# Layer 1 of a two-layer cross-attention network: probabilities laid out by head, and the prototype bias as a stacked half-precision pair

## The reference

```
x = x + tanh(g_xattn[1]) * attention(layernorm(x), ctx)   # 16 heads of 64, softmax over 77 keys
x = x + tanh(g_ffn[1]) * prototypes(layernorm(x))

def prototypes(x):                       # 32 prototypes, rank 16
    d2 = |x|^2 + |p|^2 - 2 x p^T ;  dists = sqrt(max(d2, 0))
    w = softmax(-dists / t) ;  topw, topi = top_k(w, 2) ;  topw = topw / sum(topw)
    for slot in 0, 1:
        out += topw[slot] * (A[topi[slot]] (B[topi[slot]] x) + bias[topi[slot]])
```

## Time and profile before

| | |
|---|---|
| median of three executions | 3541.69 us |
| the profiled execution | 3538.43 us |
| its span, first to last instruction | 3536.7 us |
| mean granted TensorE clock | 0.972 of full |
| TensorE busy | 3098.9 us, 88% |
| VectorE busy | 2804.7 us, 79% |
| ACT busy | 1992.0 us, 56% |
| GpSimd busy | 1969.2 us, 56% |
| last phase | from about 1819 us to the end |

### The profile page before, as it was taken

The page is one execution under the profiler, slowest core; times in us unless marked ns, Lnnn a source line. Parts: engine busy times, 40 slices in busy tenths (PEclk is TensorE's granted clock), DMA queues, the critical chain, the costliest instruction groups (busy, mean ns, idle before and its releaser), DMA issues. The chain is left out here.

```text
span 3536.7 us, 107677 instructions
## 1 busy us (share of the span) xinstructions
PE 3098.9 (88%) x35590; PEld 2626.6 (74%) x35590; DVE 2804.7 (79%) x6978; ACT 1992.0 (56%) x4103; POOL 1969.2 (56%) x3561
## 2 busy tenths in 40 slices
PE   3999994888888885999958999999999999999997
PEld 2666663666666664999947888888888888888886
DVE  5777774888888886665538898888888888888896
ACT  2666663777777774554525545555455554555553
POOL 0000003666666662000017888888888888888887
PEclk8999996999999997999979999999999999999999
DMA  3665663222232223111022323333233332333331
GB/s 118 274 247 236 248 251 98 77 82 76 75 85 76 75 82 104 36 39 48 3 67 88 99 87 100 89 96 91 88 103 89 99 90 87 103 89 99 89 88 50
DMA packets 352441, 364.00 MB, mean 103 GB/s; under 512 B 109953, under 2 KB 332673, under 8 KB 347137
## 3 DMA queue, kind: packets, MB, share of 16 engines
q1 hardware_dynamic: 338944, 333.23, 29.7%
q10 hardware_dynamic: 12960, 25.23, 1.9%
q0 software_dynamic: 160, 0.52, 0.1%
HBM read 213.11 MB, written 145.78 MB: 101 GB/s over the span
## 5 line engine op out<-in xcount | busy, mean ns | idle before, releaser
L365 POOL TENSOR_TENSOR a_probT_lo<-a_expT,a_probT_hi 128x512 f16<-128x512 f32 (+1 forms) x384 | 372.0, 997 | 244.2 <-ACT a_probT_hi L433 244.2
L933 POOL TENSOR_TENSOR a_pn<-a_prob,a_rsum 128x1232 f32<-128x1232 f32 x128 | 360.0, 2813 | 6.4 <-DVE a_rsum L1273 6.4
L1031 ACT ACTIVATE a_qT_hi<-banks 128x512 f16<-128x512 f32 x256 | 152.8, 597 | 359.0 <-PE banks L140 359.0
L138 PE MATMUL banks<-a_vo,a_probT_hi 128*128 128x256 f16 x1280 | 349.0, 273 | 2.7 <-DVE a_probT_lo L1246 2.6
L140 PE MATMUL banks<-a_vo,a_probT_lo 128*128 128x256 f16 x1280 | 348.9, 273 | 0.0
L139 PE MATMUL banks<-a_vo,a_probT_hi 128*128 128x256 f16 x1280 | 348.9, 273 | 0.0
L424 ACT ACTIVATE a_expT<-banks,a_top,w_score_scale 128x512 f32<-128x512 f32 (+1 forms) x384 | 272.2, 709 | 111.3 <-PE banks L519 111.3
L138 PE MATMUL banks<-a_xnT_hi,w_q_hi 128*128 128x256 f16 x1024 | 282.3, 276 | 4.7 <-DVE a_xnT_lo L1244 4.5
L139 PE MATMUL banks<-a_xnT_lo,w_q_hi 128*128 128x256 f16 x1024 | 282.1, 276 | 0.0
L140 PE MATMUL banks<-a_xnT_hi,w_q_lo 128*128 128x256 f16 x1024 | 282.1, 275 | 0.0
L1967 POOL PARTITION_ALL_REDUCE w_tops<-w_part_tops x1 | 0.4, 367 | 497.6 <-DVE w_part_tops L1994 497.6
(11 more groups left out here) (346 smaller groups left out, 12309.8 us busy)
## 6 DMA issues: line engine op xcount, KB each, us to landing
vo<-kv_vo_out SPq DMA_DIRECT2D x38, 2048.0 KB, 6.5
a_vo<-vo SPq DMA_DIRECT2D x64, 1152.0 KB, 5.8
kt<-kv_k_out ACTq DMA_DIRECT2D x9, 2560.0 KB, 14.6
a_k<-kt SPq DMA_DIRECT2D x64, 308.0 KB, 3.4
a_x<-in_x SPq DMA_DIRECT2D x64, 256.0 KB, 3.0
a_y<-in_x SPq DMA_DIRECT2D x64, 256.0 KB, 2.7
x<-a_y SPq DMA_DIRECT2D x64, 256.0 KB, 2.2
moe_raw<-in_L_ffn_w SPq DMA_DIRECT2D x16, 1024.0 KB, 7.4
```

The source lines that it names most:

```text
L138: nc.tensor.matmul(out, lhs[0], rhs[0], start=start, stop=False)
L365: pool.tensor_tensor(probT[b][1][0:rows, first:end, :], expT[b][0:rows, first:end, :], probT[b][0][0:rows, first:end, :], ALU.subtract).th ...
L933: pool.tensor_tensor(by_key(pn[h]), by_key(prob_of(u, h, 2)), rsum[h][:, :].unsqueeze(1).broadcast_to([P, KEYS, H]), ALU.mult).then_inc(pn ...
L1031: act.activation(out, bank[:, 0:cols].rearrange("p (c s) -> p c s", c=out.shape[1]), ACT.Copy, scale=scale)\
```

## The change

Three things are done.

1. **By head.** `prob` and `pn` hold, head after head, the first 64 keys (`first_keys`), and behind them, head after head, the last 13 (`last_keys`). The shift takes four instructions for two, `normalise` two for one; `softmax_sums` folds 64 keys to 32 and to 16 and adds the last 13, so that `quarter` has 16 x 16 elements for 19 x 16, in runs. The chunks are eight of 128 rows (two heads x 64 keys) and two of 104 rows (eight heads x 13 keys); there are no padding rows and no memsets for them. The values of a batch are loaded in two transfers of 64 partitions and eight of 13.
2. **The bias.** `wsel` is written three times side by side (96 columns), and its transpose `wselT` is in half precision: rows 0 to 63 the high half twice, rows 64 to 95 the low half, by a new subtraction on VectorE between `dots` and `add_residual`. The bias weights are a stack of high, low and high half, also 96 rows. The product is one in half precision. `layer1_weights` prepares the stack and includes the bias in the common scale.
3. **The order.** The transpose of `wsel` stands ahead of the product with the values, on TensorE and in the list of `uses`.

```diff
-            names += of(3, [("out", h)])
             names += of(7, [("wselT", h)])
+            names += of(3, [("out", h)])
...
-    by_key = lambda tile: tile[:, 0:SC].rearrange("p (k h) -> p k h", h=H)
+    first_keys = lambda tile: tile[:, 0:H * FRONT].rearrange("p (h k) -> p h k", h=H)
+    last_keys = lambda tile: tile[:, H * FRONT:SC].rearrange("p (h k) -> p h k", h=H)
...
-            sp.dma_start(vo_sb[p][:, 0:WHOLE, :, :], values(i, 0, WHOLE * P).rearrange("(c p) k d -> p c k d", p=P))\
-                .then_inc(vo_in[p], 16)
-            sp.dma_start(vo_sb[p][0:LEFT, WHOLE, :, :], values(i, WHOLE * P, LEFT)).then_inc(vo_in[p], 16)
+            for a in range(2):
+                sp.dma_start(vo_front[p][a * FRONT:(a + 1) * FRONT, :, :, :], values_front(i, a)).then_inc(vo_in[p], 16)
+            for n in range(MAIN):
+                sp.dma_start(vo_back[p][n * BACK:(n + 1) * BACK, :, :, :], values_back(i, n)).then_inc(vo_in[p], 16)
...
-            pool.tensor_tensor(by_key(pn[h]), by_key(prob_of(u, h, 2)),
-                               rsum[h][:, :].unsqueeze(1).broadcast_to([P, KEYS, H]), ALU.mult).then_inc(pn_ready, 1)
+            for keys_of, n in ((first_keys, FRONT), (last_keys, BACK)):
+                last = pool.tensor_tensor(keys_of(pn[h]), keys_of(prob_of(u, h, 2)),
+                                          rsum[h][:, :].unsqueeze(2).broadcast_to([P, H, n]), ALU.mult)
+            last.then_inc(pn_ready, 1)
...
-                if live(t - 3, NT):
-                    attend(i, t - 3, h, u, j)
                 if live(t - 7, NT):
                     need(pe, wsel_ready, t - 6)
                     bank = bank_for(i, ("wselT", h))
                     filled(nc.tensor.transpose(bank[:, 0:P], wsel[:, :], ident[:, :]), i, ("wselT", h))
+                if live(t - 3, NT):
+                    attend(i, t - 3, h, u, j)
...
-            nc.vector.reduce_sum(rsum[h][:, :], quarter[h][:, :, :].rearrange("p k h -> p h k"), AX.X).then_inc(summed, 1)
+            nc.vector.reduce_sum(rsum[h][:, :], quarter[h][:, :, :], AX.X).then_inc(summed, 1)
...
+                if live(t - 7, NT):
+                    bank, rows = full(i, ("wselT", h)), slice(2 * NPROTO, BIAS_ROWS)
+                    need(dve, wselT_hi, t - 6)
+                    nc.vector.tensor_tensor(wselT[rows, :], bank[rows, 0:P], wselT[rows, :], ALU.subtract)\
+                        .then_inc(wselT_ready, 1)
...
-                    nc.vector.tensor_tensor(wsel[:, 0:NPROTO], pick[:, 0, :], pick[:, 1, :], ALU.add)\
+                    nc.vector.tensor_tensor(wsel[:, 0:BIAS_ROWS].rearrange("p (r n) -> p r n", r=3),
+                                            pick[:, 0, :].unsqueeze(1).broadcast_to([P, 3, NPROTO]),
+                                            pick[:, 1, :].unsqueeze(1).broadcast_to([P, 3, NPROTO]), ALU.add)\
```

More of the change, by code:

```diff
@@ L731, in attention_ffn_phase @@
     rsum = [sb(f"rsum{p}", [P, H]) for p in range(2)]
-    half = sb("half", [P, 2 * QK, H])
-    quarter = [sb(f"quarter{p}", [P, QK, H]) for p in range(2)]
+    half = sb("half", [P, H, FRONT // 2])
+    quarter = [sb(f"quarter{p}", [P, H, FRONT // 4]) for p in range(2)]
     y_sb = [sb(f"y{s}", [P, D]) for s in range(SLOTS)]
@@ L1028, in split_hi @@
         def split_hi(i, use, out, cols, done, scale=1.0):
-            bank = full(i, use)
+            bank = full(i, use)[0:out.shape[0], :]
             act.activation(out, bank[:, 0:cols].rearrange("p (c s) -> p c s", c=out.shape[1]), ACT.Copy, scale=scale)\
@@ L1056, in body @@
                     if live(t - 3, NT):
-                        split_hi(i, ("probT", h, g), probT[0][:, first:end, :], (end - first) * P, probT_hi, PROB_TOP)
+                        split_hi(i, ("probT", h, g), probT[0][0:HEIGHT[g], first:end, :], (end - first) * P, probT_hi,
+                                 PROB_TOP)
                     if g == 0:
@@ L1079, in body @@
                     bank = full(i, ("wselT", h))
-                    act.activation(wselT[:, :], bank[:, 0:P], ACT.Copy).then_inc(wselT_ready, 1)
+                    act.activation(wselT[:, :], bank[0:BIAS_ROWS, 0:P], ACT.Copy).then_inc(wselT_hi, 1)
                 prep(2)
@@ L1149, in turn_probabilities @@
             first, end = GROUPS[g]
-            for c in range(first, end):
-                last = nc.tensor.transpose(bank[:, (c - first) * P:(c - first + 1) * P],
-                                           pn[1 - h][:, c * P:(c + 1) * P], ident[:, :])
+            rows = HEIGHT[g]
+            at = 0 if first < MAIN else MAIN * P
+            for c in range(end - first):
+                place = at + (first % MAIN + c) * rows
+                last = nc.tensor.transpose(bank[0:rows, c * P:(c + 1) * P], pn[1 - h][:, place:place + rows], ident[:, :])
             filled(last, i, ("probT", h, g))
@@ L1158, in attend @@
             need(pe, probT_ready, (t + 1) * PG)
-            need(pe, vo_in[p], (before + 1) * 32)
+            need(pe, vo_in[p], (before + 1) * VALUE_LOADS)
             bank = bank_for(i, ("out", h))
             for c in range(CHUNKS):
-                last = matmul3(nc, bank[:, 0:D], [x[:, c, :] for x in probT], [vo_sb[p][:, c, k, :] for k in range(2)],
+                rows = P if c < MAIN else MAIN * BACK
+                value = vo_front[p][:, c, :, :] if c < MAIN else vo_back[p][:, c - MAIN, :, :]
+                last = matmul3(nc, bank[:, 0:D], [x[0:rows, c, :] for x in probT], [value[:, k, :] for k in range(2)],
                                c == 0, c == CHUNKS - 1)
@@ L1284, in shift_scores @@
             need(dve, pn_ready, t - PROBS + 1)
[L1285 to L1290, removed]
+            tile = prob_of(u, h, 0)
+            for keys_of, first, end in ((first_keys, 0, FRONT), (last_keys, FRONT, KEYS)):
+                out, n = keys_of(tile), end - first
+                nc.vector.tensor_tensor(out[:, 0:2 * held, :].rearrange("p (b h) k -> p b h k", b=2),
+                                        both[:, :, :, first:end],
+                                        both_max.unsqueeze(3).broadcast_to([P, 2, held, n]), ALU.subtract)
+                last = nc.vector.tensor_tensor(out[:, 2 * held:H, :], third[:, :, first:end],
+                                               third_max.unsqueeze(2).broadcast_to([P, BANK_HEADS[2], n]), ALU.subtract)
+            last.then_inc(scores_read, 1)
         def prototype_products(i, t, h):
@@ L1346, in body @@
                     if live(t - 3, NT):
[L1347 to L1348 removed]
+                        split_lo(i, ("probT", h, g), probT[0][0:HEIGHT[g], first:end, :],
+                                 probT[1][0:HEIGHT[g], first:end, :], (end - first) * P, probT_hi, (t - 3) * PG + g + 1, probT_ready, PROB_TOP)
                     if g == 0:
@@ L2426, in flamingo_layers @@
                 ins["L1_ffn_B"], ins["L1_ffn_A"], ins["L1_ffn_bias"], ins["L1_ffn_temp"])
-            attention_ffn_phase(nc, layer, psum, const, batches(x1), tiles(x1), tiles(out), keys(DC, KV_COLS // P), values_out, wq, score_scale,
+            attention_ffn_phase(nc, layer, psum, const, batches(x1), tiles(x1), tiles(out), keys(DC, KV_COLS // P), (out_front, out_back), wq, score_scale,
                                 ffn)
```

88 lines of the change are left out of this document (50 added, 38 removed).

## The result

The changed kernel takes 3560.33 us (median of 3 runs, 3560.3 to 3564.03) against 3541.69: a ratio of 1.0059, 95% interval 1.0036 to 1.0081. It is slower by about 19 us. (In the later runs the kernel before had medians of 3538.6 to 3539.3, against which it would be 21.) The profiled execution took 3560.33 us with a span of 3558.5.

A forecast was written before the change was run, and what follows sets the result against it. Each batch has one stretch limited by VectorE and one by TensorE. Per batch +0.55 - 0.32 = +0.23 us, times 59 = +13.6, on 3538.4 gives 3552; the median shown is 3.3 higher, so about 3555 us, own range 3542 to 3576.

The forecast's parts named there:

- The deciding step: TensorE, h = 0: `out` takes over the bank of `xnT`, so values wait for `xnT_lo`; `yn` 0.55 us later per batch.
- The chain to `xnT_lo`: VectorE's work up to the low half of `xnT`: `rsum` 0.26 shorter, `wsel` 0.07 longer, ending at 2607.47.
- only one of two bias products counts: The bias product of h = 0 saves 0.32 us per batch; that of h = 1 only lengthens TensorE's wait, saving nothing.
- The latency from `xnT_lo` to TensorE: From the end of `xnT_lo` to the first waiting product: 0.06 us taken; 0.15 was seen after `dots`.
- the prediction's sign: In every h = 0 step the first product with the values starts 1.1 to 1.2 us after the last of `low`.
- The ends: Setup before the batches costs +1 us; at the end GpSimd may give back 1.
- GpSimd's part: Sums and `normalise` on GpSimd change by -0.15 to +0.35 us a tile, within its 1.5 us wait per batch; counted as nothing.
- SP's eight issues: Eight more issues for the values at 0.38 us add 3 us to SP's queue; no cost in time.
- That the wait doesn't hold TensorE: Rival: the wait for `xnT` does not hold TensorE; -0.84 us per batch, 3492 us; chance 0.12.
- the 50 computed: The gain if no wait for `xnT` holds TensorE: -0.84 x 59 = -50 us, giving 3492 us.
- That the two cancel: Rival: VectorE's chain is some 0.2 us shorter, so loss and gain cancel; within 7 us of 3542; chance 0.12.
- GpSimd and the values: Two rivals: GpSimd becomes the bound, about 3620 us, chance 0.05; the values come late, 3850 us, chance 0.03.

The follow-up runs named there:

- an earlier `xnT_lo`: The changed kernel, its order kept, with VectorE splitting `xnT` ahead of the maximum of the scores: 3496.83 us, ratio 0.9876.
- the pair of experiments: The changed kernel with three more bias products in each step h = 1: 3562.54 us; then in each step h = 0 instead: 3580.02 us.
- four kernels of four batches: Kernels with four batches written out in layer 1's hardware loop: before 3541.69 us, order alone 3586.50, `xnT_lo` earlier in the kernel before 3538.50, by head alone 3503.87.

## Why the prediction was right

**What held.** The deciding step: with the two uses swapped, the product with the values takes over the bank of `xnT`, once a batch, and costs more than the rest gives. Taking the order back gains 57 us, the order alone costs 47, and an earlier `xnT_lo` gives all of it back. The chain to `xnT_lo` was summed at 7.68 us behind `up` (2607.47 - 2599.79) and measured at 7.67. The parts: shift 0.95 + 0.42 + 0.31 + 0.20 = 1.88 for 1.87, `rsum` 0.41 for 0.41, `wsel` 0.25 for 0.25, the low half of `wselT` (in the prediction that of the bias weights) 0.29 for 0.28, the bias product 0.11 for 0.11. The thirty products with the values and the twelve of `q` took 4.59 for 4.58. That only one of two bias products counts was shown by the pair of experiments.

**Terms that were mis-sized.** The latency from `xnT_lo` to TensorE, taken as 0.06 from the earlier trace rows, was 0.15; the prediction had that value too, behind `dots`, and took the other. So the values start 1.26 us later and not 1.18 (1.25 behind the last product of `low`, where the prediction's sign was 1.1 to 1.2), and a batch costs 0.27 to 0.29 us and not 0.23: over 45 batches +12 us for 10.

**A term left out.** The loop's jumps. The 13 turns were counted like any batch, 13 x 0.23 = 3 us; they went from 28.02 to 28.61, 8 us. The timeline of one ordinary batch can't show it. The ends were set at nothing (+1 - 1) and came to +2. Sum for the profiled execution: 12 + 8 + 2 = 22, against 3560.3 - 3538.4 = 21.9, where 13.6 were forecast. By the medians it is 18.6, since the profiled execution before was 3.3 below its median. So the forecast of 3555 is 5 us off, and like for like it is 8: the mechanism was right and the loss was forecast too small, by terms that all err in the same direction.

**Bounds.** GpSimd's part was to change by -0.15 to +0.35 us a tile; it changed by (2.442 + 2.599) - (2.813 + 2.530) = -0.30, outside on the harmless side, and only its wait grew. `normalise` costs 1902 / 1024 = 1.86 ns an element. The Trainium skill (GPSIMD Engine Reference, section 3.1) gives 4497 / 2048 = 2.20 for a two-input `tensor_tensor` add, held back by a read port that both inputs share. By its shared port an operand that is broadcast would not be cheaper; here it was: a further element cost (1902 - 540) / 816 = 1.67 ns in `normalise`, and (1273 - 732) / 256 = 2.11 in the sums, which read two full operands, in runs too.

SP's eight issues took 8 us of its queue and not 3. They stayed hidden, as the run by head alone shows. The Trainium skill (DMA: Bandwidth & Descriptors, Rules for kernel authors) says that under 64 KB a transfer is mostly overhead; the data queue's share agrees, 33.4% for 29.7% with hardly more bytes, but this share sets nothing here.

**The rivals.** That the wait doesn't hold TensorE was wrong in the changed kernel; its price is what the order put back and the earlier `xnT_lo` measure, -36 and -42 us beside the kernel before of the same runs, against the 50 computed; inside a batch it came as computed (24.51), and the rest is at the turns and the start. That the two cancel came within 12 us of happening. GpSimd and the values were never near.

**What was not seen.** `up` waits for the new subtraction on VectorE. The prediction named what is queued behind that subtraction, not who waits for it on TensorE. In the changed kernel it ends at 2620.82, 1.2 us before `yn`, and so costs nothing; with the bias alone it takes 0.19 us of each batch.

**The parts don't add up, and why.** By head -35, bias +10, order +47: sum +22, measured +19. Inside a batch it is -0.55, -0.05, +0.79, sum +0.19, measured +0.27. By head removes the wait for `dots`, and the new order removes the same 0.52 again by being late itself; against that, the 0.26 of `rsum` counts only where TensorE waits for `xnT_lo`, and the 0.19 for which `up` waits are lost with the bias alone and not in the whole change: an estimate of 0.19 + 0.52 - 0.26 - 0.19 = 0.26.

**Open.** Why a jump costs more in one program than in another. With the single-precision bias a turn is longer than the kernel's other batches by 2.6 to 2.7 us in all four kernels of four batches; with the half-precision one by 2.9 to 4.3, where the pair that differs in the bias alone is 2.65 and 3.38 by key, 2.67 and 4.27 by head. Much of it is the clock, as shown above; why TensorE stands longer at the jump and why the clock falls more often in these programs stays open. TensorE's last work before the jump is the bias product; a page boundary that falls elsewhere is an argument from the packet counts, in windows of unequal length, and was not tried.

## What to carry to other kernels

Where buffers are handed out from a list, a moved line changes who waits for whom: for each use in the new list, look up the use that it takes over from, and compare in the timeline when that one is released with when the new owner could start. A saving counts only in front of the wait that ends last; the shift's 0.53 us was behind it, and moving one short instruction ahead of the maximum turned a loss of 19 us into a gain of 42. A sum per iteration needs a second line for the iterations that hold a jump of the loop.

## What the runs showed of the hardware

- A jump of the hardware loop costs 2.6 us in the kernel before and 2.9 to 4.3 in the kernels with the half-precision bias product; with eight batches between jumps it costs 5.4 to 6.4 there, and 2.8 in the kernel before.
- TensorE worked at 1.2 GHz behind 10 of 13 jumps after pauses of 2.2 to 2.6 us, and behind 3 of 13 after pauses of 1.4 to 1.9. With the bias alone 3.4 us at that level made a turn some 0.8 us longer (28.69 for 27.86 on average), and 6.8 us some 2.0 (29.87).
- A shift written in runs of 64 costs the same per element as one over whole rows: 948 ns for 768 elements and 415 for 256, beside 1213 for 1024 in layer 0, where the write of every sixteenth element took 1727 for 924.
- The issue of a load of 26 KB onto 13 partitions takes SP about 1 us; one of 1152 KB took 0.38.
